# An attention and FFN kernel on eight cores: the first eight weight loads issued in the block that clears the semaphores

## The chip, the cores and the metric

The kernel is one program that runs on all 8 NeuronCores of one Trainium2 chip at once. The cores form two dies of four (0 to 3, 4 to 7). The time is the device time of the slowest core in microseconds (us). The kernel before has a median of 1087.37 us over 3 runs (1086.77 to 1164.91). The profiled execution, on which all rows below rest, took 1087.49 us.

## The reference

The input is x of shape 4 x 4096 x 1024 in float32. What is computed:

```
x = x + layernorm(attention(layernorm(x)))
x = x + layernorm(ffn(layernorm(x)))

attention: batches of 2048 tokens, q, k, v from W_qkv (interleaved rows),
           softmax(q k^T / 32) v, then W_out
ffn:       (gelu(x w1 + b1) w2 + b2) * sum of the two normalised top router weights
```

## The kernel before

**The parts.** Each core takes 2048 of the query tokens and 4096 tokens as keys. The kernel does not form q and k. It first forms one matrix `am` = Wq^T Wk / 32 (1024 x 1024), and later `bm` from Wv and Wo, and works with the normalised x between them. So the first work of TensorE is the product of Wq and Wk. It takes 128 matmuls of 128x128 by 128x512: 8 row blocks, 2 halves of 512 columns, 8 chunks of the contracted side.

**The start.** The constants (line 81, in the constructor of the program) come first, then a barrier over the five engines. Then comes a block named "init" (lines 1073 to 1078), in which each engine clears its share of the 44 semaphores; line 1077 is the clear. Only then does the main block begin (line 1079), which holds all the rest, each engine with its own list of instructions in a fixed order, written out by hand. The end of the main block has the same barrier.

**The loads.** Loads with a cast from float32 to bfloat16 are issued by GpSimd (`DG`, the issuing line is 110), the small ones by SyncE (`DS`, line 108). GpSimd's list in the main block begins with loads and nothing else: for chunk c = 0 to 3, 128 rows of Wq (`wqb`, 256 KB as it lies in SBUF) and the first 512 columns of 128 rows of Wk (`wkb`, 128 KB). These eight have no wait ahead of them. Then come four `wkb` loads of the other half, then the chunks 4 to 7 with the first two tiles of x (`xn`) among them, then the other tiles of x. Each DMA of GpSimd uses the next of a ring of 24 semaphores (`yGp0` to `yGp23`), so the 25th waits for the first.

**TensorE's order in the first stage.** 32 matmuls on chunks 0 to 3 of the first half (they need just the first eight loads), 32 on chunks 0 to 3 of the other half, 32 on chunks 4 to 7 of that half, 21 on chunks 4 to 6 of the first half. That makes 117. Then eight transposes of the first x tile (line 120, with the tile `ident` that SyncE loads) and the last 11 of the 128. After that q-side products begin (`xnT` with `am`). VectorE takes the statistics of the x tiles (lines 277 to 294) and finishes `am` (lines 348, 389).

**Where the main order is made.** The class `Queues` holds one list for each engine; an entry is (waits, function, semaphore name, increment). `emit` writes the lists into the main block.

```
DG = lambda o, i, after=(): Q.dma(
    "gpsimd", lambda e, o=o, i=i: e.dma_start(o, i), after)
...
for c in range(HC):
    t_q.append(DG(wqb[:, c * H:(c + 1) * H],
                  wq[c * 128:(c + 1) * 128, :]))
    fetch_k(c, c // 4)
```

Of the kernel before, what the change touches and what calls it, by code (L numbers as in the profile page):

```python
# [19 lines left out]
NKT = 32  # L20
FF = 4096
NFC = 32
NTP = 16

ENGINES = ("sync", "gpsimd", "vector", "scalar", "tensor")
SEM_OF = {"vector": "vS", "scalar": "sS", "tensor": "tS", "gpsimd": "gS"}
RING = {"sync": ("ySy", 16), "gpsimd": ("yGp", 24)}
SEM_NAMES = (["vS", "sS", "tS", "gS"]
             + [f"ySy{i}" for i in range(16)]
             + [f"yGp{i}" for i in range(24)])  # L30
# [49 lines left out]
def build_program():  # L80
# [22 lines left out]
    Q = Queues()  # L103
# [23 lines left out]
    def at(name, cols, dt, off):  # L127
        return nc.alloc_sbuf_tensor_at(name, [128, cols], dt,
                                       offset=base + off)
# [6 lines left out]
    xn = at("xn", NKT * H, BF16, R2)  # L136
    w2b = at("w2b", NFC * H, BF16, R2)
    wqb = at("wqb", HC * H, BF16, T1)
# [109 lines left out]
    def keys(t):  # L248

        return xnT[:, t * H:(t + 1) * H].rearrange("p (c k) -> p c k", c=HC)  # L250
# [37 lines left out]
    def apply_x(u):  # L288
# [3 lines left out]
        for t in units[u]:  # L292
# [3 lines left out]
                [a])  # L296
            if t >= NTP:
                t_xT[t] = DT(keys(t), xt, [t_ln[t]])
# [443 lines left out]
    def load_x2T(g):  # L742
        war = [t_pT[NQT - 2 + g]] + t_w2[5:6] if g < 2 else [t_f1[(g - 2, NFC - 1)]]
        t_x2T[g] = DT(x2T[g % 2][:, :].rearrange("p (c t) -> p c t", t=512),
                      xns[g * 512:(g + 1) * 512, :],
                      [t_xns[4 * g + k] for k in range(4)] + war)
# [141 lines left out]
    def ffn2_part(g, k, pr, fc, hf):  # L888
# [3 lines left out]
        if fc == 0:  # L892
            aft.append(o_free.get(pr))
            if pr < 2:
# [4 lines left out]
                  w2b[:, fc * H + hf * 512:fc * H + (hf + 1) * 512],  # L899
                  fc == 0, fc == NFC - 1, aft, fc == NFC - 1)  # L900

    def ffn2(g, ks, fcs=range(NFC)):

        for fc in fcs:
            for k in ks:
                pr = pair_of(g, k)
                for hf in range(2):
                    t_f2[(4 * g + k, hf)] = ffn2_part(g, k, pr, fc, hf)
# [4 lines left out]
    def ffn2_last(cuts, banks):  # L913

        pieces = []
        for c0, c1, b in zip(cuts[:-1], cuts[1:], banks):
            o = bank[b][:, 0:c1 - c0]
            for fc in range(NFC):
                f = (fc % 16) * 512 + 384
                tok = MM(o, h1[fc // 16][:, f:f + 128],  # L920
                         w2b[:, fc * H + c0:fc * H + c1],
                         fc == 0, fc == NFC - 1,
                         [t_h1[(3, fc)], o_free[b // 2]], fc == NFC - 1)
# [61 lines left out]
    e = NQT - 1  # L985
# [85 lines left out]

    sems = {n: nc.alloc_semaphore(n) for n in SEM_NAMES}
    with nc.Block("init") as b0:
        for n, eng in enumerate(ENGINES):
            def clear(e, own=SEM_NAMES[n::len(ENGINES)]):
                for s in own:
                    e.sem_clear(sems[s])
            getattr(b0, eng)(clear)
    with nc.Block() as block:  # L1079
# [50 lines left out]
```

How the kernel before makes its waits and increments, by code:

```python
            def body(e, items=self.items[eng]):  # L66
                seen = {}
                for after, fn, name, inc in items:
                    for s, v in after:
                        if v > seen.get(s, 0):
                            e.wait_ge(sems[s], v)
                            seen[s] = v
                    ins = fn(e)
                    if name is not None:
                        ins.then_inc(sems[name], inc)
```

## Time and profile before

| | |
|---|---|
| median of 3 runs | 1087.37 us |
| the profiled execution | 1087.49 us |
| its span (slowest core, core 5) | 1085.9 us |
| spans of all cores | 1084.3 to 1085.9 us |
| TensorE matmul busy | 1064.1 us, 98% of the span |
| GpSimd busy | 101.9 us, 9% |
| mean DMA rate of the core | 102 GB/s |

The span runs from the first to the last instruction of the slowest core; 1.6 us of the execution's time lie around it. "Busy" of TensorE counts matmuls in a pipeline, whose ends are modelled. Register, branch, semaphore and DMA-issuing instructions count as not busy, except the time for which GpSimd builds a DMA's descriptors, which stands under POOL.

### The profile page before, as it was taken

To read this page: it belongs to the slowest core of one execution; us is meant where nothing else is said; L and a number is where in the kernel's file an instruction comes from. 1 tells how busy PE (TensorE), PEld (TensorE's weight loads), DVE (VectorE), ACT (ScalarE), POOL (GpSimd) and SP (SyncE) were. 2 spreads that over 40 slices of the span, in tenths; PEclk is the share of its full clock that TensorE was granted. 3 is DMA by queue.
4 is the path that set the end of the run, shared out by engine and by line. 5 is a ranking of instruction groups with operands and counts; after the bars stand their busy time and mean duration, and the time that the engine had idled before them with its cause. 6 is when DMAs were issued, how large, how long until landed. Compare 5 with 4: busy or idle time off the path is not lost.

```text
span 1085.9 us, 14321 instructions; the slowest of 8 cores (1084.3 to 1085.9 us)
## 1 busy us (share of the span) xinstructions
PE 1064.1 (98%) x5288; PEld 495.7 (46%) x5288; DVE 350.4 (32%) x723; ACT 315.1 (29%) x516; POOL 101.9 (9%) x175
## 2 busy tenths in 40 slices
PE   5999999999999999999999999999999999999996
PEld 2654444444444444444444444444444444444444
DVE  0673842333433333334332322006103300330033
ACT  1474432323332223233322323203520242023300
POOL 7430000000000000000000320001000000000000
PEclk9999999999999999999999999999999999999999
DMA  8999994443244444433349999985202220220012
GB/s 121 161 183 172 173 225 85 107 101 83 80 78 96 98 107 107 98 83 80 80 88 150 166 165 195 162 161 115 80 1 78 75 43 1 70 73 13 1 46 71
DMA packets 154980, 110.57 MB, mean 102 GB/s; under 512 B 119712, under 2 KB 130208, under 8 KB 154912
## 3 DMA queue, kind: packets, MB, share of 16 engines
q0 software_dynamic: 31120, 62.94, 29.4%
q1 hardware_dynamic: 123792, 46.72, 22.1%
q8 instruction: 43, 0.70, 0.3%
q14 instruction: 25, 0.20, 0.1%
HBM read 88.69 MB, written 25.17 MB: 105 GB/s over the span
## 4 chain that ended last, share of the span: by engine, by line
PE 94%; DMA 2%; DVE 1%; POOL 1%; issue 1%; ACT 1%; POOLq 0%; DVEq 0%; ACTq 0%
PE pAll L116 94%; DMA xn<-xo 2%; POOL wkb L110 1%; PE pAll L120 0%; POOL wqb L110 0%; ACT xnT L327 0%; DVE st L277 0%; DVE st L279 0%; DVE am L389 0%; ACT qst L466 0%; DVE yt L978 0%; ACT rsa L284 0%; DVE nma L290 0%; POOLq L1079 0%; DVE xn L294 0%
## 5 line engine op out<-in xcount | busy, mean ns | idle before, releaser
L116 PE MATMUL pAll<-xnT,qt 128*128 128x512 bf16 x1024 | 225.1, 379 | 0.0
L116 PE MATMUL pAll<-xn,pT 128*128 128x512 bf16 x1024 | 223.6, 379 | 0.0
L116 PE MATMUL pAll<-x2T,w1b 128*128 128x512 bf16 x1024 | 222.6, 379 | 0.0
L116 PEld LDWEIGHTS pAll<-xnT,qt 128*128 128x128 bf16 x1024 | 100.2, 98 | 120.8 <-issue 0.5
L116 PEld LDWEIGHTS pAll<-xn,pT 128*128 128x128 bf16 x1024 | 100.2, 98 | 120.8
L116 PEld LDWEIGHTS pAll<-x2T,w1b 128*128 128x128 bf16 x1024 | 99.8, 98 | 120.0 <-issue 0.6
L597 DVE TENSOR_REDUCE nmx<-pAll 128x1 f32<-128x1024 f32 x64 | 78.0, 1222 | 177.0 <-PE pAll L116 177.0
L603 ACT ACTIVATE pb<-pAll,nmx 128x1024 bf16<-128x1024 f32 x64 | 71.3, 1114 | 167.6 <-DVE nmx L597 167.5
L116 PE MATMUL pAll<-w2b,h1a 128*128 128x512 bf16 (+1 forms) x528 | 113.2, 373 | 0.2 <-issue 0.2
L116 PE MATMUL pAll<-w2b,h1b 128*128 128x512 bf16 (+1 forms) x528 | 113.0, 373 | 0.0
L974 ACT ACTIVATE x2r<-x2r,nm 128x1024 f32<-128x1024 f32 x15 | 17.2, 1147 | 214.4 <-DVE nm L972 214.4
L116 PEld LDWEIGHTS pAll<-w2b,h1a 128*128 128x128 bf16 x528 | 51.6, 98 | 59.5 <-issue 0.6
L116 PEld LDWEIGHTS pAll<-w2b,h1b 128*128 128x128 bf16 x528 | 51.6, 98 | 58.9
L945 DVE TENSOR_TENSOR yt<-pAll,b2b 128x1024 f32<-128x1024 f32 (+2 forms) x18 | 19.9, 1104 | 180.7 <-PE pAll L116 180.7
L841 ACT ACTIVATE h1b<-pAll,b1f 128x512 bf16<-128x512 f32 x64 | 43.2, 687 | 60.0 <-PE pAll L116 59.9
L116 PE MATMUL pAll<-xnT,am 128*128 128x512 bf16 (+2 forms) x392 | 58.5, 305 | 0.7 <-ACT xnT L327 0.7
L116 PE MATMUL pAll<-bm,uT 128*128 128x512 bf16 x256 | 57.9, 379 | 0.0
L841 ACT ACTIVATE h1a<-pAll,b1f 128x512 bf16<-128x512 f32 x64 | 42.8, 685 | 50.1 <-PE pAll L116 50.1
L658 ACT CAST ub<-pAll 128x1024 bf16<-128x1024 f32 x16 | 16.2, 1012 | 119.5 <-PE pAll L116 119.5
L116 PE MATMUL pAll<-wkb,wqb 128*128 128x512 bf16 x128 | 30.0, 394 | 12.2 <-DMA wkb<-wk 12.0
L116 PEld LDWEIGHTS pAll<-xnT,am 128*128 128x128 bf16 x392 | 31.2, 98 | 22.9 <-issue 1.1
L110 POOL DMA_DIRECT2D x2s<-xf x16 | 8.7, 545 | 345.6 <-DVE xf L719 345.6
(91 smaller groups left out, 601.1 us busy)
## 6 DMA issues: line engine op xcount, KB each, us to landing
xf<-xo POOLq DMA_DIRECT2D x16, 512.0 KB, 4.6
x2s<-xf POOLq DMA_DIRECT2D x16, 512.0 KB, 2.9
w1b<-w POOLq DMA_DIRECT2D x8, 1024.0 KB, 22.4
w2b<-w POOLq DMA_DIRECT2D x8, 1024.0 KB, 60.1
x2r<-x2s POOLq DMA_DIRECT2D x16, 512.0 KB, 4.7
y<-yt SPq DMA_DIRECT2D x15, 512.0 KB, 2.7
xn<-xo POOLq DMA_DIRECT2D x16, 256.0 KB, 30.4
xn<-xr POOLq DMA_DIRECT2D x16, 256.0 KB, 49.7
```

The source lines that it names most:

```text
L110: "gpsimd", lambda e, o=o, i=i: e.dma_start(o, i), after)
L116: e.matmul(o, l, m, start=f, stop=s), after, sig)
L597: mx = V(lambda e: e.tensor_reduce(n, pair[pr], AX, ALU.max, negate=True), [tok, t_cf.get(i - 2)])
L603: lambda e: e.activation(o, pair[pr], AF.Exp, bias=n, accum_out=l),
L658: t_ub[i] = A(lambda e: e.copy(o, pair[2]), [t_ctx[i], t_uT.get(i - 2), t_qs[NQT - 1]])
L841: lambda e: e.activation(o, bank[b], AF.Gelu_apprx_tanh, bias=b1f[:, fc:fc + 1]),
L945: a = V(lambda e, c=c, acc=acc: e.tensor_tensor(o[:, c], acc, b2b[:, c], ALU.add), [done, t_b2] + war)
L974: a = A(lambda e: e.activation(x[:, :], x[:, :], AF.Identity, bias=n_), [t_n, t_x2r[t]])
```

## The change

The eight first entries of GpSimd's list are taken out of it and issued in the "init" block, behind GpSimd's clears. GpSimd clears the eight semaphores of these loads (`yGp0` to `yGp7`) and no others. The other 36 semaphores are split over SyncE, VectorE, ScalarE and TensorE, nine each. The loads, their semaphores, their order and all waits on them are as before. The barrier at the end of the "init" block stays where it is, and so does the main block behind it.

```diff
+NEARLY = 8
...
     with nc.Block("init") as b0:
-        for n, eng in enumerate(ENGINES):
-            def clear(e, own=SEM_NAMES[n::len(ENGINES)]):
-                for s in own:
+
+        own = {eng: SEM_NAMES[n::4] for n, eng in enumerate(
+            ("sync", "vector", "scalar", "tensor"))}
+        early = [name for _, _, name, _ in Q.items["gpsimd"][:NEARLY]]
+        own = {eng: [s for s in o if s not in early] for eng, o in own.items()}
+
+        def first_loads(e):
+            for s in early:
+                e.sem_clear(sems[s])
+            for after, fn, name, inc in Q.items["gpsimd"][:NEARLY]:
+                assert not after
+                fn(e).then_inc(sems[name], inc)
+            del Q.items["gpsimd"][:NEARLY]
+
+        b0.gpsimd(first_loads)
+        for eng, names in own.items():
+            def clear(e, names=names):
+                for s in names:
                     e.sem_clear(sems[s])
             getattr(b0, eng)(clear)
```

## Rows read from the trace of the kernel before

**Rows 1.** The page: the span and the busy times of the engines.

```profile
span 1085.9 us, 14321 instructions; the slowest of 8 cores (1084.3 to 1085.9 us)
...
PE 1064.1 (98%) x5288; PEld 495.7 (46%) x5288; DVE 350.4 (32%) x723; ACT 315.1 (29%) x516; POOL 101.9 (9%) x175
```

**Rows 2.** Windows, core 5: us, busy (x instructions), clock, DMA share, GB/s.

```profile
2.80:6.80 4.00, 0.00 (x0) 0.00 (x0) 0.00 (x0) 1.23 (x2) 3.97 (x8) 1.00 0.57 44
6.80:14.80 8.00, 5.18 (x16) 1.88 (x17) 0.00 (x0) 0.00 (x0) 8.00 (x16) 1.00 1.05 143
14.80:19.80 5.00, 3.56 (x17) 1.52 (x17) 0.93 (x2) 1.18 (x3) 5.00 (x11) 1.00 1.08 154
63.00:1078.00 1015.00, 1014.45 (x4892) 466.22 (x4890) 318.28 (x651) 292.33 (x470) 60.24 (x102) 1.00 0.49 99
```

**Rows 3.** The chain that ended last, in order of time: start us, us, what.

```profile
2.22 0.61 issue
2.83 0.69 POOL wqb L110
...
15.45 24.08 DMA xn<-xo
...
42.80 0.13 DVE am L389
```

**Rows 4.** TensorE on core 5 in order of time, with the wait before each piece.

```profile
9.62 7.10 PE L116 MATMUL pAll<-wkb,wqb 128*128 128x512 bf16 x24 [9.62 <-DMA wkb<-wk]
18.15 20.54 PE L116 MATMUL pAll<-wkb,wqb 128*128 128x512 bf16 x93 [1.44 <-DMA wkb<-wk]
...
40.19 2.53 PE L116 MATMUL pAll<-wkb,wqb 128*128 128x512 bf16 x11 [0.97 <-DMA wkb<-wk]
```

**Rows 5.** Init block, by line: duration ns min/median/max, first and last start us.

```profile
L1077 POOLq EVENT_SEMAPHORE_RANGE_CLEAR  x9: 44/44/48, 1.0 to 1.6; - x9
...
L1077 PEldq EVENT_SEMAPHORE_RANGE_CLEAR  x8: 56/56/63, 1.1 to 2.0; - x8
...
L1073 POOLq DRAIN  x1: 41/41/41, 1.7 to 1.7; - x1
L1073 PEldq DRAIN  x1: 8/8/8, 2.1 to 2.1; - x1
L1073 PEldq EVENT_SEMAPHORE  x1: 51/51/51, 2.3 to 2.3; - x1
```

**Rows 6.** GpSimd's issues from the timeline, core 5.

```profile
6.64 2.72 POOL L110 DMA_DIRECT2D wkb<-wk  x5
```

**Rows 7.** The eighth load alone (`wkb`, issued at 6.64): issue to landing, core 5.

```profile
DMA to landing us min/median/max: 11.4/11.4/11.4
```

**Rows 8.** GpSimd's DRAINs at lines 81 and 1079, the memset and the operation before them.

```profile
0.58 0.12 POOL L81 MEMSET const-uint8-127<- 128x1 uint8 x1
L81 POOLq DRAIN  x1: 182/182/182, 0.6 to 0.6; - x1
1079.53 0.68 POOL L962 TENSOR_TENSOR rs<-ve,mhalf 128x1 f32<-128x1 f32 x1 [11.66 <-DVE ve L960]
L1079 POOLq DRAIN  x1: 2835/2835/2835, 1079.5 to 1079.5; - x1
1080.31 0.21 DVE L969 TENSOR_SCALAR sr<-rs,sc 128x1 f32<-128x1 f32 x1
```

**Rows 9.** TensorE on cores 0 and 1 in order of time.

```profile
9.20 3.57 PE L116 MATMUL pAll<-wkb,wqb 128*128 128x512 bf16 x8 [9.20 <-DMA wkb<-wk]
...
38.71 0.61 PE L120 MATMUL pAll<-ident,xn 128*128 128x128 bf16 x8
...
9.07 8.18 PE L116 MATMUL pAll<-wkb,wqb 128*128 128x512 bf16 x24 [9.07 <-DMA wkb<-wk]
```

**Rows 10.** Span of core 0, with its mean granted clock.

```profile
core 0: 1085.0 us, clock 0.998
```

**Rows 11.** ScalarE's table load, from the timeline.

```profile
2.54 1.28 ACT L211 ACT_TABLE_LOAD   x1 [2.54 <-DVE mhalf L210]
```

## The prediction

> **What bounds the kernel.** I read the page first. TensorE is busy for 1064.1 of 1085.9 us [rows 1]. The windows then say where the other 22 us are. From 63 to 1078 us TensorE is busy for 1014.45 of 1015.00 us [rows 2], so nothing is to be had there, and whatever moves its beginning moves the end by the same amount. The idle time lies ahead of 63 us. TensorE on core 5 does nothing until 9.62 us, waits 1.44 us before 18.15 and 0.97 us before 40.19, each time for a DMA of Wk [rows 4]. The chain of waits agrees: it begins with GpSimd's first issue at 2.83 us and then stands for 24.08 us in one DMA [rows 3]. From 6.8 us on the DMA engines are full [rows 2], and TensorE keeps catching up with them. The change lies at the head of this.
>
> **Moved: the first load starts earlier.** GpSimd's clears run from 1.0 to 1.6 us, and then it sits at the barrier until TensorE, which is slower at clearing, has drained at 2.1 [rows 5]. Its release is at 2.22 and its first load stands at 2.83, 0.61 us later [rows 3]. With the change it has eight clears instead of nine, 0.07 us apart, the last ending near 1.57. If the same 0.61 follows, the first load starts at 2.18: **0.65 us earlier**. Bounds: 0 if the 0.61 has another cause that stays in place, 1.26 (2.83 - 1.57) if the dispatch itself costs nothing. I take 0.65, because the 0.61 is the only row of such a start. The DMA engines are full and the eight loads are queued up, so all eight land earlier by this.
>
> **Added: nine clears on each of the other four.** TensorE has 8 now, 0.12 us apart [rows 5], so 0.12 us more. This lies under GpSimd's issuing and costs nothing. If GpSimd were quick it would cost nothing still: it issues until after 6 us.
>
> **Added: the barrier now stands behind eight loads.** This is where I decide. The eight issues are 0.54 us apart (6.64 for the eighth, 2.83 for the first [rows 3, 6]), so the descriptors are built by 2.18 + 3.81 + 0.6 = 6.6 us. Then comes GpSimd's DRAIN, and no engine passes before it ends. How long does a DRAIN of GpSimd take with loads in flight? No row shows one. The nearest rows: at line 1073 it took 41 ns with no DMA ever issued [rows 5]. At line 81 it ended 0.05 us after the last memset (0.6 + 0.18 against 0.58 + 0.12), also with no DMA ever issued. At line 1079, where GpSimd has issued DMAs, it took 2835 ns from 1079.5, though the one operation ahead of it ended at 1080.21: **2.1 us beyond its own work** [rows 8]. The operation's result had been used by VectorE by 1080.31, so it was not that [rows 8]. So after DMAs, a DRAIN of GpSimd does something more, and the thing it has left to ask about is its DMA queues. All its loads had landed long before there; here eight are in flight. The lower end is 0.05 us past 6.6; the upper end is the landing of the eighth load plus 2.1 us. I take the landing of the eighth load plus nothing, because a DRAIN that looks at the queues is likely to wait until they are empty, and its own 2.1 us can run while the loads fly.
>
> **The sum under that reading, core 5.** The eighth load lands 11.4 us after its issue at 6.64, at 18.04 [rows 6, 7]; minus 0.65 is 17.4. From the last report to TensorE's release took 0.2 us in the old barrier (2.1 to 2.3, rows 5's events), so TensorE may go at 17.65, and its first matmul starts at **17.7 instead of 9.62**. It has all of chunks 0 to 3 then and will not wait for them. Two paces are in the rows: 93 matmuls in 20.54 us are 0.221 each [rows 4], the first 8 on core 0 took 3.57, or 0.446 each [rows 9]. The ratio is two, so the second is the lower clock level, 1.2 GHz. 24 matmuls in 7.10 us (core 5) solve to 8 at 0.446, 24 in 8.18 (core 1) to 13 [rows 4, 9]. The low-clock stretch comes after the first matmul wherever that is, so it is paid again and not more. 117 matmuls need 117 x 0.221 + 8 x 0.225 = 27.7 us, or 28.8 with 13 of them, and end at 45.4 to 46.5 where they ended at 38.69 [rows 4]: **+6.7 to +7.8 us**.
>
> **Is a load then late?** GpSimd's ninth load goes out at 17.65 + 0.61 = 18.3 instead of about 7.2. The queue before it has run dry. After the very first issue, 0.18 MB had moved by 6.8 us, four microseconds later (44 GB/s [rows 2]); at 154 GB/s that is 1.1 us of work, so a restart costs about 2.9 us and the stream resumes in effect at 21.2. The eight loads are 4 x 256 + 4 x 128 KB, 1.57 MB. In the old order the stream passed this point at 16.4: the windows add up to 1.32 MB at 14.8 (4 us at 44 GB/s and 8 us at 143), and the rate was then 154 GB/s [rows 2]. So **the DMA stream is 4.8 us late**. The last Wk load, awaited at 40.19, comes at 45.0 and TensorE asks for it at 46.0 or later: the wait of 0.97 us is gone [rows 4]. The x tile that landed at 39.53 (15.45 + 24.08, rows 3) lands at 44.3; its statistics need 1.4 us, and `am` is not ready for line 389 before 48. TensorE is the later of the two, and every step after it (line 389 at 42.80, rows 3) moves with TensorE.
>
> So core 5 moves by 6.7 - 0.97 = **5.7 us, or 6.8** with the longer low-clock stretch. Core 0 had no such wait before its eight transposes at 38.71; it starts at 17.3 and its 117 end at 45.0 to 46.1: +6.3 to +7.4 on a span of 1085.0 [rows 9, 10]. Both give a span of 1091.3 to 1092.7, and the slowest of eight cores is near the upper end: 1092.2. The profiled execution lies 1.6 us over its span and 0.12 over the median. 1092.2 + 1.6 - 0.1 = **1093.7 us**.
>
> **Costs at nothing.** ScalarE's table load (1.28 us) moves from 2.54 to about 18, and its first real use is behind the 25th matmul, 24 us by then [rows 11]. SyncE's load of `ident` goes out at 17.7 and is wanted at 45. VectorE's two memsets are wanted later still. With the cover gone they would cost under 2 us.
>
> **Rival 1: the DRAIN ends with the descriptors (or 2.1 us after).** Then the barrier opens at 6.7, at the latest at 8.7 + 0.2; TensorE's first data are there at 8.97, and nothing but the 0.65 remains. The ninth load goes out at 7.3 (9.5 at the latest), while the queue has work until 15.7. For it: in the trace the issue of a load ends long before its landing (0.60 us against 11.4), and 2.1 us is a number of its own, with nothing in flight. Time: 1087.4 - 0.65 = **1086.7 us**. A page speaks for this one: the Trainium skill, Perfetto Trace Analysis, section "DMA Instruction — SWDGE (GPSIMD)", has a GpSimd load finish on its DSPs once the descriptors are written, and the DMA engines carry on by themselves. By that rule a DRAIN has nothing more to wait for and the time would be 1086.7; the row at line 1079 does not settle it, since nothing was in flight there.
>
> **Rival 2: the DRAIN waits and then adds its 2.1 us.** Then everything of the main sum is 2.1 us later: **1095.8 us**. It belongs to the upper end of the forecast's own range.
>
> **Rival 3: no earlier start.** The 0.61 us were not the dispatch, or the first load waits in its place for something else, and the change only puts the barrier behind the loads: 1093.7 + 0.65 = **1094.3 us**.
>
> **How the numbers follow.** Forecast with rival 2 as its upper end 0.85 (of which rival 2 has 0.1), rival 1 0.12, rival 3 0.03. Rival 1 keeps that much because the 2.1 us stand in one row, taken with no load in flight; it gets no more because the same engine's two DRAINs without DMAs behind them had nothing of the kind. The forecast's own range: at the lower end the first load gains 1.26 instead of 0.65, the low-clock stretch is the short one, and the slowest core is moved as little as core 5 (5.7 - 0.6): 1087.4 + 5.1 = 1092.5, less 1.7 since a queue without followers may land its last load sooner (the eighth load's last 0.1 MB took from 16.4 to 18.04), so 1090.8. At the upper end rival 2 with a long low-clock stretch, 1096.5. 1090.8 to 1096.5 leaves out rival 1 and a little over: 0.8. The bound for telling a difference is 2%, 21.7 us, and no case comes near: a slowdown of that size would need a stall of nearly twice the eighth load's 11.4 us. Faster 0.01, same 0.98, slower 0.01.
>
> **What would show it.** In the profile after: GpSimd's first load near 2.2 us (the moved step); its DRAIN in the init block lasting from about 6 to 17 us (the decision; if it ends before 9, rival 1 holds); TensorE's first matmul near 17.7 with no DMA wait in the next 32; the ninth load at about 18.3; a hole in the DMA rate between 17 and 21 us; no wait at the last Wk load; 63 to 1078 us unchanged but for the shift. Wrong would be a first matmul near 9.0, or one near 17.7 with the end moved by less than 4 us, which would mean that the idle time between 43 and 63 us gives something back.

## The result, and the profile after

The changed kernel takes 1093.74 us, median of 4 runs (1093.63 to 1093.84), against 1087.31 us for the kernel before on the same chip. The ratio is 1.006, with a 95% interval of 1.0047 to 1.0074: **slower by 6.4 us**. That is clear of the noise, and far inside the 2% that the forecast took as its bound for telling a difference. The forecast was 1093.7. The profiled execution took 1093.63 us. Medians here and below are over all executions; the ratios leave out those in which the cores of a die ran at a lower granted clock, so that the two can differ a little.

The page of the kernel after, its head: the span, the busy times and, from its fifth part, the row of the first matmuls with busy, mean ns and the idle time before them.

```profile
span 1092.1 us, 14321 instructions; the slowest of 8 cores (1090.4 to 1092.1 us)
...
PE 1065.5 (98%) x5288; PEld 496.3 (45%) x5288; DVE 350.2 (32%) x723; ACT 315.0 (29%) x516; POOL 102.0 (9%) x175
...
L117 PE MATMUL pAll<-wkb,wqb 128*128 128x512 bf16 x128 | 31.5, 411 | 16.9 <-PEq L1074 16.7
```

The instructions are as many as before, and the busy times differ by 1.4 us for TensorE and by 0.6 or less for the others [rows 1] (another core is the slowest, see below); the span is 6.2 us longer. Nearly all of TensorE's idle time ahead of these matmuls, 16.7 of 16.9 us, is now ended by its own sequencer at line 1074, the init block. The row names no DMA. The same lines of code stand one line lower in the kernel after (line 1073 is 1074, 110 is 111, 116 is 117), and two lines lower in the kernel with the DRAIN alone (110 is 112, 116 is 118).

The DRAINs and barrier events of the init block, core 6 (the slowest), with duration in ns and start in us:

```profile
L1074 PEldq DRAIN  x1: 8/8/8, 2.2 to 2.2; - x1
L1074 POOLq DRAIN  x1: 11035/11035/11035, 5.1 to 5.1; - x1
...
L1074 PEldq EVENT_SEMAPHORE  x1: 51/51/51, 16.3 to 16.3; - x1
```

GpSimd's DRAIN took 41 ns at this place before [rows 5] and takes 11035 ns now. TensorE has been drained since 2.2 us and is released at 16.3. The timeline of GpSimd on the same core (start, duration, what, and the idle time before it) shows what lies ahead of the DRAIN and behind it, and the second fence is the landing of the load at 5.93:

```profile
2.13 0.69 POOL L111 DMA_DIRECT2D wqb<-wq  x1 [1.43 <-DVEq L1074]
...
5.93 0.60 POOL L111 DMA_DIRECT2D wkb<-wk  x1
16.81 2.12 POOL L111 DMA_DIRECT2D wkb<-wk  x4 [10.27 <-POOLq L1074]
```

```profile
L111 POOL DMA_DIRECT2D wkb<-wk x1: 603/603/603, 5.9 to 5.9; - x1
...
DMA to landing us min/median/max: 9.8/9.8/9.8
```

The eighth load lands at 5.93 + 9.8 = 15.7. The DRAIN ends at 5.1 + 11.0 = 16.1, 0.4 us after it, and the ninth load goes out at 16.81. TensorE in order of time, first on core 6, then on core 5, whose rows of before are [rows 4]:

```profile
16.72 29.16 PE L117 MATMUL pAll<-wkb,wqb 128*128 128x512 bf16 x117 [16.72 <-PEq L1074]
45.81 0.61 PE L121 MATMUL pAll<-ident,xn 128*128 128x128 bf16 x8
46.26 2.54 PE L117 MATMUL pAll<-wkb,wqb 128*128 128x512 bf16 x11
```

```profile
16.84 24.44 PE L117 MATMUL pAll<-wkb,wqb 128*128 128x512 bf16 x102 [16.84 <-PEq L1074]
41.44 3.40 PE L117 MATMUL pAll<-wkb,wqb 128*128 128x512 bf16 x15
...
45.21 2.54 PE L117 MATMUL pAll<-wkb,wqb 128*128 128x512 bf16 x11
```

The first matmul on core 5 stood at 9.62 and stands at 16.84. From there on TensorE waits for no load on these two cores. The 1.44 us before its 25th matmul and the 0.97 us before the last 11 are gone. The last 11 move from 40.19 to 45.21. One core of the eight still waits for a load, core 3, for 0.25 us before its last 11:

```profile
44.78 2.53 PE L117 MATMUL pAll<-wkb,wqb 128*128 128x512 bf16 x11 [0.25 <-DMA wkb<-wk]
```

The windows of core 6 (us, busy and instructions of PE, PEld, DVE, ACT and POOL, then granted clock, DMA share, GB/s) show the hole in the stream of loads, one low clock, and the rest of the kernel:

```profile
6.00:14.00 8.00, 0.00 (x0) 0.00 (x0) 0.00 (x0) 0.00 (x0) 0.54 (x2) 1.00 1.06 137
14.00:18.00 4.00, 1.28 (x4) 0.49 (x5) 0.10 (x2) 1.39 (x2) 1.19 (x3) 1.00 0.40 68
18.00:19.00 1.00, 1.00 (x4) 0.41 (x3) 0.00 (x0) 0.10 (x1) 1.00 (x3) 1.00 0.45 42
...
29.00:34.00 5.00, 5.00 (x22) 2.07 (x20) 0.00 (x0) 0.00 (x0) 4.73 (x9) 0.84 1.04 139
...
68.00:1083.00 1015.00, 1014.82 (x4891) 466.33 (x4892) 318.96 (x652) 293.48 (x472) 60.46 (x103) 1.00 0.48 99
```

Between 14 and 19 us the DMA engines are busy for less than half, where they were full before [rows 2]. Behind 68 us nothing has changed: TensorE is busy for 1014.82 of 1015.00 us [rows 2]. In every kernel of this study the time from the start of TensorE's last matmul of the first stage to the end of the span is 1043.6 to 1043.8 us (mean over the cores; 1043.8 before, 1043.8 after). So where the first stage ends tells all that there is to tell of a kernel here, and that is before 53 us on every core.

Mean over the eight cores, us:

| | before | after | later by |
|---|---|---|---|
| first load issued | 2.83 | 2.13 | -0.70 |
| first matmul | 9.40 | 16.97 | 7.57 |
| eight transposes | 38.35 | 44.85 | 6.50 |
| last matmul of the stage | 41.31 | 47.50 | 6.19 |
| end of the span | 1085.13 | 1091.31 | 6.18 |

### The profile page after: what moved, and what is told of

Read it like the earlier page. It is cut to its first block, busy times and chain, and to the rows that moved or that the text cites. A ratio compares the mean times of both kernels' runs of the same rounds, so it can differ in the third digit from the quotient of the medians.

```text
span 1092.1 us, 14321 instructions; the slowest of 8 cores (1090.4 to 1092.1 us)
## 1 busy us (share of the span) xinstructions
PE 1065.5 (98%) x5288; PEld 496.3 (45%) x5288; DVE 350.2 (32%) x723; ACT 315.0 (29%) x516; POOL 102.0 (9%) x175
## 4 chain that ended last, share of the span: by engine, by line
PE 96%; DVE 1%; ACT 1%; issue 0%; POOLq 0%; DVEq 0%; ACTq 0%
PE pAll L117 96%; PE pAll L121 0%; ACT xnT L328 0%; DVE st L278 0%; DVE st L280 0%; DVE am L390 0%; ACT qst L467 0%; DVE yt L979 0%; ACT rsa L285 0%; DVE nma L291 0%; DVE am L349 0%; POOLq L1095 0%; DVE xn L295 0%; DVE st L949 0%; DVE yt L946 0%
## 5 line engine op out<-in xcount | busy, mean ns | idle before, releaser
L117 PE MATMUL pAll<-wkb,wqb 128*128 128x512 bf16 x128 | 31.5, 411 | 16.9 <-PEq L1074 16.7
```

Source lines behind the costliest of these rows:

```text
L117: e.matmul(o, l, m, start=f, stop=s), after, sig)
```

## The experiments

Two theories stood at the start. **Theory A**, the forecast's: GpSimd's DRAIN at the end of the block waits until the loads in flight have landed. That holds back all five engines, and by it the first matmuls and the ninth load. **Theory B**: the loss comes from something else that moved, the clears or the loads that now have no followers, and the DRAIN is only where it shows. The last four runs size single terms. Each kernel is given by its difference from the kernel that is named.

### The block's end without GpSimd's DRAIN

Against the kernel after; the barrier and its events stay.

```diff
-    with nc.Block("init") as b0:
+    with nc.Block("init", no_gpsimd_drain=True) as b0:
```

> The changed kernel, but the init block ends without GpSimd's DRAIN; the barrier itself (four reports, one release) stays. Theory (the DRAIN waits for the eight loads to land): the barrier opens near 5.3 us, TensorE's first matmul comes near 8.9 on the data, the ninth load goes out at 6.5 to 7.3 and the DMA queue never runs dry; 1086.6 us, 0.7 less than before and 7.1 less than the changed kernel. Rival (the barrier behind eight issues costs the time by itself, or the early issue does): still 1092 to 1094 us.

Measured: 1087.25 us over 11 runs, before 1087.43; ratio 0.9998 (0.9988 to 1.0007). GpSimd's events at the block's end, and TensorE, core 0:

```profile
L1074 POOLq EVENT_SEMAPHORE  x2: 17/17/17, 5.1 to 5.2; - x2
```

```profile
8.23 6.53 PE L117 MATMUL pAll<-wkb,wqb 128*128 128x512 bf16 x16 [8.23 <-DMA wkb<-wk]
...
17.76 17.15 PE L117 MATMUL pAll<-wkb,wqb 128*128 128x512 bf16 x76 [0.83 <-DMA wkb<-wk]
...
39.75 2.54 PE L117 MATMUL pAll<-wkb,wqb 128*128 128x512 bf16 x11 [0.75 <-DMA wkb<-wk]
```

The barrier opens at 5.2 instead of 16.3, and the whole 6.4 us are gone: the DRAIN was the loss. The head start of the loads brought nothing at the end of the stage in the trace; the interval of the times, -1.3 to +0.8 us, would by itself allow the 0.7 that were expected. The first matmul starts at 7.97 instead of 9.40 (mean over cores), and the last matmul of the stage starts at 41.42 instead of 41.31. The gain is used up on the way. The second load lands 1.4 us earlier than before (mean), the eighth 0.2 earlier (17.5 against 17.7), the twentieth at 31.4 (31.3) and the last Wk load at 39.05 (39.0). TensorE's row above shows the other end of it: it waits 0.75 us for that last load.

### The DRAIN alone

Against the kernel before: all loads stay in the main block, and a DRAIN stands in GpSimd's list behind the eighth. The other engines do not wait for it.

```diff
-                for after, fn, name, inc in items:
+                for n, (after, fn, name, inc) in enumerate(items):
+                    if eng == "gpsimd" and n == 8:
+                        e.drain()
```

> The kernel before, with one DRAIN put into GpSimd's list of the main block behind the eighth load; no other engine is held. Theory: the DRAIN ends at the eighth load's landing (about 16.8, 10.2 us after its issue at 6.64), the ninth load goes out at 17.4, the DMA stream is about 4.4 us late and TensorE, which starts at 9.6 as before, now waits for loads up to the last of Wk near 44.5: 1091.9 us (1091 to 1093). Rival A (the late start of TensorE is all of the loss, the dry queue is hidden): 1087 to 1088. Rival B (a DRAIN of GpSimd has a fixed 2.1 us and does not look at the loads): the ninth load goes out at about 9.5 and the time is 1087.3.

Measured: 1092.92 us, ratio 1.0046 (1.003 to 1.0063). GpSimd's ninth load on core 5, then its DRAIN, then TensorE:

```profile
17.90 2.12 POOL L112 DMA_DIRECT2D wkb<-wk  x4 [10.67 <-issue]
```

```profile
L70 POOLq DRAIN  x1: 11612/11612/11612, 5.8 to 5.8; - x1
```

```profile
9.47 9.58 PE L118 MATMUL pAll<-wkb,wqb 128*128 128x512 bf16 x32 [9.47 <-DMA wkb<-wk]
21.94 13.93 PE L118 MATMUL pAll<-wkb,wqb 128*128 128x512 bf16 x56 [2.88 <-DMA wkb<-wk]
...
45.21 2.53 PE L118 MATMUL pAll<-wkb,wqb 128*128 128x512 bf16 x11 [1.33 <-DMA wkb<-wk]
```

The DRAIN behaves the same with no block's end near it. The eighth load lands at 17.0 on this core and the DRAIN ends at 5.8 + 11.6 = 17.4; on each of the eight cores it ends 0.37 us after the landing. TensorE begins as before, runs out of loads at its 33rd matmul, and waits again for the last Wk load, 1.33 us. That load lands at 44.1 instead of 39.0 (mean). So **a pause of the load queue alone costs 5.0 us** (by the ratio). There is a second effect in it. The windows of core 5 behind the 2.88 us wait:

```profile
22.00:24.00 2.00, 2.00 (x5) 0.70 (x6) 0.00 (x0) 0.00 (x0) 2.00 (x5) 0.50 0.75 51
24.00:26.00 2.00, 2.00 (x8) 0.61 (x6) 0.00 (x0) 0.00 (x0) 2.00 (x5) 0.79 1.01 154
26.00:28.00 2.00, 2.00 (x11) 0.87 (x10) 0.00 (x0) 0.00 (x0) 2.00 (x5) 1.00 1.11 193
```

The granted clock is 0.50 from 22 to 24 us, which is 1.2 GHz: 5 matmuls in 2 us where there are 11 in the third row. TensorE still had to wait for later loads here, the last one 1.33 us, so it cost little: core 3, the only one whose clock did not fall, ended at 1089.8 us, the others at 1089.8 to 1090.4.

### TensorE held back alone

Against the kernel before: nothing is moved, but the first matmuls also wait for the eighth load (`t_k[0][3]`).

```diff
-                            [t_q[c], t_k[0][c]] if i == 0 else ())
+                            [t_q[c], t_k[0][c], t_k[0][3]] if i == 0 else ())
```

> The kernel before, with one more wait on TensorE's first matmul: the eighth load. GpSimd's issues are as before, so the queue never runs dry. Theory: the first matmul comes at 17.6 to 18.1, 117 matmuls run without a wait and end 6.1 to 7.5 us late; 1094.2 us (1093 to 1095.5). Rival (the dry DMA queue is what costs in the changed kernel, TensorE would catch up): 1087 to 1089.

Measured: 1094.61 us, ratio 1.0063 (1.0047 to 1.0079). TensorE on core 4, the slowest:

```profile
18.14 24.97 PE L116 MATMUL pAll<-wkb,wqb 128*128 128x512 bf16 x102 [18.14 <-DMA wkb<-wk]
...
47.03 2.54 PE L116 MATMUL pAll<-wkb,wqb 128*128 128x512 bf16 x11
```

A late start of TensorE costs 6.9 us (by the ratio) with the stream untouched. **The two halves do not add up**: 5.0 and 6.9 by themselves, 6.5 together. The mean last matmul of the stage says the same: later by 5.2, 7.3 and 6.2 us. TensorE's late start hides the late stream (0.25 us on one core is the only wait for a load that is left), and the change's start is about a microsecond earlier than here (first matmul 16.97 against 17.93 mean).

### The clears alone

Against the kernel after: the clears are split as there, and all loads go back to the main block.

```diff
-            for after, fn, name, inc in Q.items["gpsimd"][:NEARLY]:
-                assert not after
-                fn(e).then_inc(sems[name], inc)
-            del Q.items["gpsimd"][:NEARLY]
```

> The changed kernel's split of the clears (GpSimd eight, the other four nine each), with all loads in the main block as before. Theory: TensorE's ninth clear moves the barrier by 0.12 us, so 1087.4 us, no difference that can be told. Rival (the new split is part of the loss): more than 1 us slower.

Measured: 1087.32 us over 12 runs, ratio 1.0001 (0.9992 to 1.001). GpSimd, core 0:

```profile
2.94 0.69 POOL L111 DMA_DIRECT2D wqb<-wq  x1 [2.24 <-POOLq L1074]
```

TensorE's ninth clear delays the barrier, and with it the first load, by 0.11 us (2.83 before), at no cost. This rules out the clears. The first experiment rules out the early issue by itself: it keeps the clears and the early loads and has no loss. Nor do loads without followers land later: in the kernel with the DRAIN alone the eighth took 10.2 us (mean), against 11.0 before. So theory B falls.

### Two loads early

Against the kernel after: `NEARLY = 2`.

```diff
-NEARLY = 8
+NEARLY = 2
```

> The changed kernel with two loads moved into the init block instead of eight. Theory: GpSimd's DRAIN ends 0.37 us after the second load's landing (near 7.0, so 7.4), TensorE's first matmul comes at about 7.7, earlier than before (9.4), and so TensorE's start costs nothing; but the third load goes out at 8.1 onto a queue that is dry, the stream is 2.8 us late, and TensorE waits for it again: about 1090.0 us (1089 to 1091.5). Rival (what costs is TensorE's late start alone): 1087. Rival (the loss is a fixed price of loads ahead of the barrier): 1093.7.

Measured: 1092.69 us, ratio 1.0044 (1.0027 to 1.006). The forecast of 1090.0 (1089 to 1091.5) missed. The three runs behind the ratio took 1090.32, 1092.23 and 1093.15, the last of them the profiled one. The DRAIN on core 4, the slowest, and TensorE there:

```profile
L1074 POOLq DRAIN  x1: 4928/4928/4928, 2.1 to 2.1; - x1
```

```profile
7.60 3.42 PE L117 MATMUL pAll<-wkb,wqb 128*128 128x512 bf16 x8 [7.60 <-PEq L1074]
12.31 1.89 PE L117 MATMUL pAll<-wkb,wqb 128*128 128x512 bf16 x8 [1.30 <-DMA wkb<-wk]
16.64 2.71 PE L117 MATMUL pAll<-wkb,wqb 128*128 128x512 bf16 x8 [2.44 <-DMA wkb<-wk]
21.89 23.45 PE L117 MATMUL pAll<-wkb,wqb 128*128 128x512 bf16 x93 [2.53 <-DMA wkb<-wk]
```

The last Wk load came 2.8 us later than before (mean), as expected. The miss is elsewhere: the last 93 matmuls take 23.45 us where the same 93 took 20.54 before [rows 4]. The windows of core 4 say why:

```profile
17.50:20.00 2.50, 1.86 (x5) 0.40 (x3) 0.00 (x0) 0.00 (x0) 2.50 (x6) 0.51 0.78 104
...
22.00:27.80 5.80, 5.80 (x14) 1.91 (x13) 2.77 (x4) 2.39 (x4) 4.75 (x9) 0.50 1.10 159
27.80:33.00 5.20, 5.20 (x26) 2.35 (x25) 0.00 (x0) 0.00 (x0) 1.05 (x2) 1.00 1.12 173
```

After waits of 1.30 and 2.44 us with eight matmuls between, the granted clock fell to 0.50 at 17.6 and stayed there until 27.8; a third wait, of 2.53 us, lies in that time. 14 matmuls took 5.80 us, 0.414 each; then 26 took 5.20, 0.200 each. Fourteen matmuls at 0.2 us more are the 2.9 us. The other seven cores had the full clock for good from 17.1 to 22.1 us on and ended at 1086.8 to 1089.8 us; core 4 ended at 1091.6. Over the cores the last matmul of the stage is 3.6 us later than before (mean), so the slowest core adds over a microsecond to what the late stream costs on the average one.

### Twelve loads early

Against the kernel after: `NEARLY = 12`.

```diff
-NEARLY = 8
+NEARLY = 12
```

> The changed kernel with twelve loads moved instead of eight (2.1 MB instead of 1.57). Theory: the DRAIN ends 0.37 us after the twelfth landing, near 19.2; TensorE's first matmul at about 19.6, 2.6 us later than with eight, and TensorE is the bound: 1096.3 us (1095.3 to 1097.5). Rival (a fixed price): 1093.7.

Measured: 1097.71 us, ratio 1.0098 (1.0081 to 1.0115); 1.4 us above the forecast and 0.2 above its range. The DRAIN and TensorE, core 4:

```profile
L1074 POOLq DRAIN  x1: 14047/14047/14047, 7.1 to 7.1; - x1
```

```profile
21.73 23.68 PE L117 MATMUL pAll<-wkb,wqb 128*128 128x512 bf16 x102 [21.73 <-PEq L1074]
```

The direction and the mechanism are as expected. The twelfth load, issued at 8.3, landed at 20.1 to 21.0 (mean 20.4), over a microsecond later than reckoned; the first matmul stands at 21.51 (mean) and not at 19.6. With 2, 8 and 12 loads ahead of it the DRAIN takes 4.9, 11.0 and 14.0 us, and ends at 7.0, 16.1 and 21.2: it follows the last landing, not a constant. What it adds behind the landing grows with the number of loads: 0.12, 0.37 and 0.53 us, the same on all eight cores to 0.002 us. With no load it took 0.041 [rows 5], so in this range it is 0.041 us, and 0.041 more for each load.

### SyncE's two loads early

Against the kernel before: SyncE clears the semaphores of its two small loads (`ident`, `b1f`) first and issues both in the init block; GpSimd's loads stay.

```diff
             def clear(e, own=own, eng=eng):
                 for s in own:
                     e.sem_clear(sems[s])
+                if eng == "sync":
+                    for after, fn, name, inc in Q.items["sync"][:2]:
+                        assert not after
+                        fn(e).then_inc(sems[name], inc)
+                    del Q.items["sync"][:2]
```

> The kernel before, with SyncE's two small loads (the transpose identity and a bias) issued in the init block behind SyncE's clears; GpSimd's list is untouched. If SyncE's DRAIN does not wait for landings: it lasts under 0.1 us, the barrier opens by 2.6 at the latest (two issues of 0.4 us behind the clears), GpSimd's first load stands at 2.83 to 3.2, and the time is 1087.3 us. If every engine's DRAIN waits for its own DMAs: it ends near 5, and the first load goes out about 2.5 us later, 1089 to 1090 us.

Measured: 1087.49 us over 10 runs, ratio 1.0002 (0.9993 to 1.0012). SyncE's DRAIN at the block's end, then the later of its two loads with its time to landing, then GpSimd's first load, core 6:

```profile
L1073 SPq DRAIN  x1: 127/127/127, 2.6 to 2.6; - x1
```

```profile
L108 SPq DMA_DIRECT2D b1f<-b1r x1: 421/421/421, 2.1 to 2.1; - x1
...
DMA to landing us min/median/max: 1.8/1.8/1.8
```

```profile
3.44 0.69 POOL L110 DMA_DIRECT2D wqb<-wq  x1 [2.73 <-POOLq L1073]
```

SyncE's DRAIN ends at 2.7 (it takes 127 ns, and 7 in the kernel after, where no load is ahead of it), and its load lands at 2.1 + 1.8 = 3.9. So **waiting for the landing belongs to GpSimd's DRAIN and its loads**, and not to every DRAIN. GpSimd's first load stands at 3.44, 0.61 later than before and 0.24 beyond what was expected, and that costs nothing: the last matmul of the first stage starts at 41.43 (41.31). Together with the first experiment, the start of the first load may lie anywhere from 2.13 to 3.44 us without a measurable effect.

## Why the prediction was right

The sum came out at 1093.7 and 1093.74 was measured. Its mechanism was shown, but three of its terms were mis-sized and partly cancelled: the eighth load's time to landing was taken 1.5 us too long, the way from there to the first matmul 0.65 us too short, the lateness of the stream 0.5 us too large. TensorE started about a microsecond earlier than forecast, and the slowest core still ended where it was put. That the two numbers agree to 0.1 us is luck.

- **Which bound decides the end: right.** Everything behind 68 us moved unchanged with TensorE [rows 2].
- **Moved: first load 0.65 us earlier: right in size, worth nothing.** It came 0.70 earlier, and it follows GpSimd's own clears: 1.71 us with two of them, 2.13 with eight, 2.42 with twelve, 0.07 for each. The sum credits the gain to every landing; in the change it does shift the eighth landing. Without the DRAIN it is used up before the stage ends. So the trace does not bear out rival 1's price of 1086.7 even for a kernel without the wait; 1087.25 was measured, with an interval that does not exclude it. Rival 3, no earlier start, fell with the 0.70.
- **The clears: right.** Nothing, by the fourth experiment.
- **The decision, that the DRAIN waits for the eighth load and adds nothing: right, but for 0.37 us.** By so much it ends after the landing, on all eight cores. The 2.1 us by which the DRAIN at line 1079 outlasts its operation [rows 8] were no share of it; that DRAIN still takes 2.8 us. It stands behind all 145 DMAs of GpSimd, and 0.041 us for each would make 6 us of it, so its cause is open. Rival 2 fell with this. Rival 1 fell as well: the Trainium skill, Perfetto Trace Analysis, section "DMA Instruction — SWDGE (GPSIMD)", has the load's instruction end with its descriptors, and the trace agrees for the load (0.60 us, landing after 9.8), but what follows for a DRAIN does not hold here.
- **First matmul at 17.7: a microsecond too late.** Measured 16.84 on core 5 and 16.97 as a mean. The eighth load landed at 15.9 on core 5, not at 17.4. I took its time to landing from the kernel before, 11.4 us [rows 7], where more loads were issued behind it all the time; it was 9.9 here and 9.8 to 10.4 over the cores. The range had allowed 1.7 us for this, the sum nothing. The experiments agree: in the kernel with the DRAIN alone, which also has no followers, it was 10.2 (mean; 9.7 to 10.6), and with followers (TensorE held back) 11.2 (10.6 to 11.9). Against that, TensorE needed 1.0 us from the landing to its first matmul, where I had 0.3: 0.4 for the DRAIN's end, 0.2 for the barrier, 0.4 from the release at 16.3 to the matmul at 16.72.
- **117 matmuls in 27.7 or 28.8 us: right in the main.** Core 5 took from 16.84 to 44.84, 28.0; core 0 27.6; the six cores without a dip of the clock 27.1 to 28.5. Core 6 took 29.2: its granted clock was 0.81 from 28.9 to 33.3 us (mean 0.84 in the window from 29 to 34), which no core had in the trace of before, and which gives 0.8 us. Cores 6 and 7 had this. On core 6 that dip gave back most of the microsecond of the earlier start: without it core 6 would have ended at 1091.3, and core 1, at 1091.7, would have been the slowest. It does not explain the time of the kernel, though: in the other three executions the slowest cores ended at 1092.2 to 1092.3 us, and on a core that ended last in each the mean granted clock was 0.998, against 0.997 on core 6 here.
- **The stream is 4.8 us late, and hidden: too large by 0.5.** 5 MB had been moved at 42.7 against 38.4 (means), so 4.3; the ninth load went out at 16.8 and not at 18.3, and landed after 3.9 us. The last Wk load landed at 42.7 to 44.6, on seven cores before TensorE asked for it; only on core 3, where it came last, did TensorE wait 0.25 us. The wait of 0.97 us on core 5 went, as predicted. What the prediction didn't say is how much this cover was worth. A late stream alone costs 5.0 us: most of the loss has two sufficient causes here.
- **Core 5 by 5.7 to 6.8, core 0 by 6.3 to 7.4: both a little too much.** Measured 5.5 and 6.0, 0.2 and 0.3 below the lower ends. The slowest core, put near the upper end at 1092.2, was another one, at 1092.1.
- **The costs at nothing** (table load, `ident`, memsets): none of them appears among the waits before the first matmul of `xnT`.

What is open: why the head start of 0.7 us is lost by the eighth load. In the kernel without the DRAIN the bytes stay ahead (5 MB at 37.7 against 38.4, means) while the landings that TensorE waits for do not, and no run here separates what delays them. Open too is why the DRAIN's time behind the landing grows with the number of loads. Nor is it shown what let the granted clock dip on cores 6 and 7.

## What to carry to other kernels

Look at what closes the block before moving a load of GpSimd into it: here its DRAIN waited until the load had landed, and the barrier handed that wait to every engine, so both TensorE's start and the next load's issue were set by the landing of the last load moved. Two loads, 384 KB, were enough for 4.8 us. A head start at the mouth of a full queue may be worth nothing, as the 0.7 us were here; ask for the landing of the last load that the slow engine waits for, not for the first. Where both a late start and a late stream are in play, the larger one hides the other, so that mending either alone gives little (with the start alone mended, 5.0 of the 6.5 us would have been lost still; with the stream alone mended, 6.9 were lost): undo their common cause.

## What the hardware did that I had not expected

- A DRAIN of GpSimd behind loads in flight lasted 4.9, 11.0 and 14.0 us with 2, 8 and 12 loads, ending 0.12, 0.37 and 0.53 us after the last landing; SyncE's DRAIN behind two loads of its own ended in 127 ns, 1.2 us before the landing.
- The same load, the eighth, landed sooner with nothing queued behind it: 9.8 to 10.4 us, against 10.4 to 11.4 in the kernel before (means 10.1 and 11.0).
- A queue that had run dry took 3.9 us from the first new issue to its landing, and the DMA engines' share was still 0.45 between 1.2 and 2.2 us after that issue.
- The granted clock fell back to 0.50 after short waits of TensorE early in the kernel: after 1.30 and 2.44 us of waiting, with eight matmuls between, for 10 us on one core (two loads early), and around 2.88 us of waiting for some 3 us on another (the DRAIN alone). It did not do so each time: on core 3 of the kernel with the DRAIN alone it stayed at 1.00 through waits of 2.61 and 1.69 us. After one long wait at the start, in the changed kernel, all 117 matmuls ran without such a fall on all cores, but for the 0.81 on two.
